# Input loads moved from SyncE's queue to ScalarE's, one batch's stacks sent later, and the idle matmuls placed behind a wait

## What is computed

```
xn = layernorm(x)
q, k, v = xn @ Wq.T + bq, ctx @ Wk.T + bk, ctx @ Wv.T + bv      # 16 heads of 16
z = softmax(q k^T) v  per head
x = x + layernorm(z + xn) * gamma + beta
f = layernorm(x);  f = f + mixture_of_experts(layernorm(f))      # 8 experts, top 2 of a softmax router
x = x + f
```

## Time and profile before

| | |
|---|---|
| median of three executions | 836.14 us (835.61 to 837.38) |
| profiled execution, and its span | 837.38 us, 835.5 us |
| TensorE busy | 752.3 us, 90% |
| VectorE busy | 629.9 us, 75% |
| ScalarE busy | 564.1 us, 68% |
| GpSimd busy | 536.1 us, 64% |
| DMA | 104.43 MB, mean 125 GB/s |
| chain that ended last | TensorE 58%, DMA 12%, VectorE 9%, GpSimd 6%, SyncE's queue 5% |

### The profile page before, as it was taken

One profiled execution on the slowest core, in us unless ns is written; L12 is line 12 of the kernel. 1 busy time (PEld: TensorE's weight loads), 2 busy tenths in 40 slices (PEclk: granted clock), 3 DMA queues, 4 the chain that ended last, 5 costly groups with the idle time before them and its releaser, 6 DMA issues.

```text
span 835.5 us, 26294 instructions
## 1 busy us (share of the span) xinstructions
PE 752.3 (90%) x8080; PEld 587.7 (70%) x8081; DVE 629.9 (75%) x1781; ACT 564.1 (68%) x1469; POOL 536.1 (64%) x609
## 2 busy tenths in 40 slices
PE   7888989999999999999999997555979888999994
PEld 4565666767777777777777674435878777999994
DVE  7688998989989999989999897784366763445441
ACT  3466767878888888888888785334565544666662
POOL 5433657767768767777777674335656555777773
PEclk9999999999999999999999999755989998999998
DMA  8566665777786786877877868511334323443341
GB/s 216 145 142 163 151 149 125 176 167 153 163 180 153 172 173 148 184 151 165 180 152 164 193 126 206 165 21 43 61 56 59 58 40 58 70 70 58 62 66 18
DMA packets 154001, 104.43 MB, mean 125 GB/s; under 512 B 68365, under 2 KB 149561, under 8 KB 153817
## 3 DMA queue, kind: packets, MB, share of 16 engines
q1 hardware_dynamic: 135502, 79.47, 43.3%
q0 software_dynamic: 10944, 14.10, 10.6%
q10 hardware_dynamic: 7498, 10.18, 4.1%
HBM read 36.65 MB, written 17.33 MB: 65 GB/s over the span
## 4 chain that ended last, share of the span: by engine, by line
PE 58%; DMA 12%; DVE 9%; POOL 6%; issue 6%; SPq 5%; ACT 2%; DVEq 1%; ACTq 0%; POOLq 0%
PE s_row L1004 9%; PE pj L899 7%; PE s_row L913 7%; PE zt L945 6%; PE s_t L933 6%; PE pj L868 6%; PE pj L1015 4%; PE zt L1015 4%; SPq L660 3%; DMA out_x<-index_space,idx_s 3%; DVE negmax L1390 2%; DMA q_stack<-m_part 2%; PE pj L886 2%; DMA zscr<-zn 2%; DMA stack_x<-k_part 2%
## 5 line engine op out<-in xcount | busy, mean ns | idle before, releaser
L1390 DVE TENSOR_REDUCE negmax<-s_row 100x1 f32<-100x361 f32 x512 | 250.9, 522 | 23.6 <-PE s_row L913 19.3
L1209 ACT ACTIVATE p_t<-s_t 128x400 f32<-128x400 f32 x384 | 188.0, 499 | 82.1 <-PE s_t L933 74.3
L913 PE MATMUL s_row<-stack_x,q_stack 125*128 125x361 bf16 x512 | 132.5, 319 | 16.5 <-DVE negmax L1390 8.6
L730 POOL DMA_INDIRECT out_x<-index_space,idx_s x57 | 91.3, 1601 | 77.1 <-ACT index_space L1194 35.4
L933 PE MATMUL s_t<-q_stack,stack_x 128*128 128x100 bf16 x1536 | 129.4, 211 | 11.0 <-ACT p_t L1209 7.9
L933 PEld LDWEIGHTS s_t<-q_stack,stack_x 128*128 128x128 bf16 x1536 | 94.5, 99 | 56.1 <-issue 31.3
L1004 PE MATMUL s_row<-w_qkv,v_aug 128*128 128x128 f32 x912 | 117.9, 285 | 1.7 <-DVE v_aug L1485 1.7
L1004 PEld LDWEIGHTS s_row<-w_qkv,v_aug 128*128 128x128 f32 x912 | 113.2, 202 | 2.3 <-DVE v_aug L1485 2.2
L1395 DVE TENSOR_SCALAR p_t<-p_t 128x1200 f32<-128x1200 f32 x128 | 100.8, 787 | 11.4 <-ACT p_t L1209 11.3
L899 PE MATMUL pj<-w_qkv,ct 128*128 128x256 f32 x384 | 104.8, 395 | 0.3 <-ACT k_rest L1130 0.3
L945 PE MATMUL zt<-p_t,v_aug 128*32 128x100 f32 (+1 forms) x3072 | 96.3, 260 | 0.8 <-DVE p_t L1395 0.8
(11 more groups left out here) (244 smaller groups left out, 1413.9 us busy)
## 6 DMA issues: line engine op xcount, KB each, us to landing
stack_x<-k_part SPq DMA_DIRECT2D x192, 192.0 KB, 3.6
q_stack<-q_part SPq DMA_DIRECT2D x192, 64.0 KB, 2.0
ct<-in_ctx_t SPq DMA_DIRECT2D x32, 361.0 KB, 4.3
stack_x<-in_w ACTq DMA_DIRECT2D x8, 512.0 KB, 6.4
w_s<-in_w ACTq DMA_DIRECT2D x14, 256.0 KB, 3.0
zscr<-zn SPq DMA_DIRECT2D x32, 100.0 KB
z_in<-zscr SPq DMA_DIRECT2D x32, 100.0 KB
zf_d<-zf_s SPq DMA_DIRECT2D x32, 100.0 KB
```

The costliest lines, as they stand in the source:

```text
L730: pool.indirect_dma_start(out_rows[0:n], bass.IndirectOffsetOnAxis(idx_s[:, k.slot:k.slot + 1], 0), ys[:, k.slot, :], None, bounds_check=n ...
L913: nc.tensor.matmul(s_row[h % 2][:, 0:KEYS], q_stack[0:MROW, b.slot, h, :], k_stack[0:MROW, b.slot, h, 0:KEYS], start=True, stop=True).then ...
L1209: nc.scalar.activation(p_t[:, quad % 2, kt, :], s_t[g % 2][:, 0:4 * Q], ACT.Exp).then_inc(exp_done, 1)
L1390: v.tensor_reduce(negmax[:, b.slot, h:h + 1], s_row[h % 2][0:Q, 0:KEYS], AXIS.X, ALU.max, negate=True).then_inc(max_done, 1)
```

## The change

Four edits. (1) The x loads 2 to 5 get the sizes 10, 3, 4 and 3 batches and are issued by ScalarE, in the slots (iteration, slot) = (-1, 8), (0, 2), (0, 8), (1, 2), ahead of what ScalarE has in that slot. (2) `first_stacks` sends batch 0 only; batch 1 goes by the places of SP like the later ones, in slot 2 of iteration -1. (3) The first key half of batch 0 goes to `pj[1]` instead of `s_t[0]`. (4) The idle matmuls write `tr` instead of `s_t[1]`, and TensorE's wait for the four memsets stands ahead of them.

```diff
-X_LOADS = [slice(0, FIRST), slice(FIRST, 12), slice(12, 17), slice(17, 22), slice(22, 27), slice(27, B)]
-X_LOAD_BEHIND = {1: 2, 2: 3, 3: 4, 4: 5}
+X_LOADS = [slice(0, FIRST), slice(FIRST, 12), slice(12, 22), slice(22, 25), slice(25, 29), slice(29, B)]
+X_LOAD_AT = {(-1, 8): 2, (0, 2): 3, (0, 8): 4, (1, 2): 5}
...
-                return (s_t[0], zt)[t] if a.known and a.index == 0 else pj[1]
+                return zt if a.known and a.index == 0 and t == 1 else pj[1]
...
-                def x_load(k):
-                    sp.dma_start(x_all[:, X_LOADS[k], :], x.rearrange("b q d -> q b d")[:, X_LOADS[k], :]).then_inc(x_loaded[k], 16)
-
-                def first_stacks(b):
+                def first_stacks():
...
-                for b in range(2):
-                    first_stacks(b)
-                x_load(X_LOAD_BEHIND[1])
+                first_stacks()
...
-                            if w.known and w.index < 2:
+                            if w.known and w.index == 0:
...
-                            if w.known and w.index in X_LOAD_BEHIND:
-                                x_load(X_LOAD_BEHIND[w.index])
...
-                        nc.tensor.matmul(s_t[1][:, 0:G * Q], zt_s[:, 0:128], zt_s[:], start=True, stop=True)
+                        nc.tensor.matmul(tr[:, 0:G * Q], zt_s[:, 0:128], zt_s[:], start=True, stop=True)
...
+                pe.wait_ge(memsets, 4)
                 pe.wait_ge(zeros_ready, 1)
                 run_idle(8)
-                pe.wait_ge(memsets, 4)
...
+                        if isinstance(turn, int) and (i, s) in X_LOAD_AT:
+                            k = X_LOAD_AT[i, s]
+                            act.dma_start(x_all[:, X_LOADS[k], :], xv[:, X_LOADS[k], :]).then_inc(x_loaded[k], 16)
```

More of the change, by code:

```diff
@@ L594, in _ @@
                 sp.wait_ge(pad_written, 3)
-                def x_load(k):
-                    sp.dma_start(x_all[:, X_LOADS[k], :], x.rearrange("b q d -> q b d")[:, X_LOADS[k], :]).then_inc(x_loaded[k], 16)
-                def first_stacks(b):
+                def first_stacks():
                     for part, (q_made, k_made, q_count, k_count) in enumerate(((qh_ready, kh_ready, 2, 2), (qm_ready, km_ready, 1, 1), (q_low_ready, k_low_ready, 1, 1))):
-                        sp.wait_ge(k_made, k_count * (b + 1))
+                        sp.wait_ge(k_made, k_count)
                         for g, p in enumerate(PROD):
                             if p == part:
-                                sp.dma_start(k_stack[g:ROWS:len(PROD), b].rearrange("r h k -> r (h k)"),
-                                             k_part[:, b, p].rearrange("p t k -> p (t k)")).then_inc(k_stacked[b], 16)
-                        sp.wait_ge(q_made, q_count * (b + 1))
+                                sp.dma_start(k_stack[g:ROWS:len(PROD), 0].rearrange("r h k -> r (h k)"),
+                                             k_part[:, 0, p].rearrange("p t k -> p (t k)")).then_inc(k_stacked[0], 16)
+                        sp.wait_ge(q_made, q_count)
                         for g, p in enumerate(QPART):
                             if p == part:
-                                sp.dma_start(q_stack[g:ROWS:len(PROD), b].rearrange("r h k -> r (h k)"),
-                                             q_part[:, b, p].rearrange("p t k -> p (t k)")).then_inc(q_stacked[b], 16)
-                for b in range(2):
-                    first_stacks(b)
-                x_load(X_LOAD_BEHIND[1])
+                                sp.dma_start(q_stack[g:ROWS:len(PROD), 0].rearrange("r h k -> r (h k)"),
+                                             q_part[:, 0, p].rearrange("p t k -> p (t k)")).then_inc(q_stacked[0], 16)
+                first_stacks()
                 def later_loads():
```

## The result

The changed kernel takes 846.01 us (median of six, 842.66 to 849.81) against 835.88 us of the kernel before beside it: ratio 1.0109, 95% interval 1.0087 to 1.0132. It is slower, by 9 to 10 us; the forecast was 838.2 us and the range ended at 842.0. The profiled execution after took 848.3 us, its span is 846.4 us, 10.9 us more than before. The work is the same: TensorE 751.0 us busy, VectorE 631.4.

What follows compares the result with a forecast made beforehand. The prediction took TensorE's pace to bound the kernel from about 140 us, so the first 110 us decide: 5.2 us later, 3.1 us regained, 836.14 + 2.1 = 838.2 us against the median; range 833.7 to 842.0 us.

Steps and rivals of the forecast that it cites:

- Idle matmuls behind the memsets: Kernel start: idle matmuls begin 3.94 us later, part comes back; 1.1 us late taken, ends 0 and 3.9.
- Batch 1's stacks: Before iteration 0: six key transfers wait for the low key part and land at 40 to 41, 3 to 4 us late.
- x load 2: Iteration 0 slot 1: VectorE gets the 1000 KB load at 44.9 instead of 39.68; 5.2 us late, earlier lateness included.
- The other loads: From 53.2 to 107 us: VectorE's x waits go and SP's queue is freed; 3.1 us gained, between 1 and 6.4.
- rival (d): Iteration 1: loads interleave with batch 2's stacks too, TensorE waits one more microsecond, 1 us back; 841.3 us; chance 0.07.
- (c): Start: the clock falls at batch 1 and load 2 lands at 46.3 or later; 840.9 us; chance 0.13.
- (a): Start: iteration 0's idle time, the zn store and `m_part` make delay and gain cancel; 836.1 us; chance 0.24.
- (b): Start: freeing SP's queue gains 6.4 us, load 2 lands early, stacks cost 3 us; 832.7 us; chance 0.14.
- The sum: Whole kernel: 837.38 + 5.2 - 3.1 = 839.5 us against the profiled execution, 838.2 us against the median; chance 0.42.

Runs made afterwards that it cites:

- the base: The kernel before with one difference: GpSimd's wait before a scatter in the second part takes its value by a load with bounds; ratio 0.9993 (0.9966 to 1.0020).

## Why the prediction was wrong

The direction was right and the size was not: 2.1 us were forecast, 10 came. By its steps:

- **Idle matmuls behind the memsets.** Right. Keys at 12.68 (forecast 12.9), the two subtractions 1.56 and 0.57 us, batch 1's key matmuls 1.40 us, lateness 0.5 us where 1.1 was forecast. The 1.3 us that the clock was to give back are 2.66 - 1.38 us, at a clock of 0.50 and at the full one; it did, with 1.40 us at 1.00. That the shorter gap kept the clock up is not shown: the base kept it too, with a gap of 1.70 us and no edit there.
- **Batch 1's stacks.** This step failed. It put the landing of the stacks at 40 to 41 us, with 1 to 2 us for the load and the context beside them. It was 46.7.
- **x load 2.** The sum of bytes was 2 to 3 us short: 43.9 us and 1 us to the semaphore, against 46.7 for the last of the stacks. No run shows that 1 us by itself: in the profile after, packets of SP's queue pass until 46.8 us and the rows start at 46.81. What failed is who waits. The step let VectorE's statistics, due at 39.68, wait for the load. In fact the load was the first to be through (its queue is empty after 44 us) and the stacks the last, and these are due at 37.35. The term was 5.2 us; it measured 46.81 - 37.35 = 9.5. Of the 4.3 us of error 2.3 are the earlier due time and the rest the later end.
- **Why the stacks were last.** The packets of both queues pass side by side, 271 of ScalarE's and 134 of SP's in 36 to 38 us of the profile after, and in the run with edit 1 alone even one 64 KB transfer was held for 8.9 us. Together they make a share of 1.12 until 40 us, and then only 0.75 and 0.69; with the load cut into 96 and 4 partitions the share stays at 1.1 until 44 us and 1.8 us come back. The prediction had the load beside the stacks, but gave that only the 1 to 2 us, and it let all bytes pass at the 231 GB/s of the earlier trace rows, where 185, 167 and 147 GB/s passed in the three stretches of 2 us from 40 us on.
- **The other loads.** VectorE's waits at 56, 72 and 78 us went, and iterations 2 and 3 gave back 2.9 us where 3.1 were forecast for all three. That the numbers agree is luck in part: half of the 3.1 was to come from the wait of 1.56 us in iteration 1, and that iteration takes 16.80 us where it took 16.77, since the clock of 0.90 cost the 1.3 us that the wait gave back. And iteration 0 lost 3.7 us: 3.0 of idle time, with a second wait of 3.05 us, and 0.7 of busy time at the lower clock. The prediction had no term for either. So the four iterations take 70.3 us, 0.9 more than the 69.5 before, where it wanted some 3 less. The second wait is rival (d), which had 0.07 and was priced at one microsecond; that loads beside batch 2's stacks hold them up was right (with loads 3 to 5 behind the stacks no wait of over 0.3 us is left there). (c) had the jam in view but capped the delay at 6.6 us, from twice the landing time of a load of half the size that was queued behind the stacks.
- **Rivals (a) and (b)** needed load 2 to land early or to be absorbed. Neither happened; the delay passed to the end undiminished, 10.5 us at batch 6 and 10.9 in the span.
- **The sum** with the measured terms: 9.7 + 3.7 - 2.9 = 10.5 us, and 0.4 in the rest.

Open: why the second wait was 3.05 us in one execution and 1.43 in another, and how much of the 10 us each edit makes by itself.

## What to carry to other kernels

In this kernel the large load that is not urgent does best on the queue of the urgent transfers, behind them, in a stretch in which the DMA engines are idle (0.9970 with each load one stack earlier); on another queue it is not behind them but among them (a wait of 8.68 us, and of 0.92 us with the load behind the stacks on SP's queue). What is issued behind it on its own queue waits for it in turn, as `m_part` did for 8.20 us, so the size has to fit the gap. When two transfers run together, cost both: ask which is through last, and whose consumer is due first. After a delay has been priced, ask also what its idle time does to TensorE's clock: here it was at 0.50 after 8.68 us of waiting, and the 197 matmuls of iteration 1 took 1.3 us longer at a mean of 0.90.

## What the runs showed of the hardware

With both queues in use, ScalarE's queue passed 271 packets to SP's 134 in 36 to 38 us and 165 to 163 in 38 to 40 us of the profile after; the ratio is not fixed, and why it changes is not shown. In bytes it was 0.28 to 0.18 MB and then 0.17 to 0.23 MB. And the same kernel start kept the full clock in one execution and lost it in another (1.40 and 2.66 us for four key matmuls), which moved `m_part` of batch 4 by 1.0 us. After a long wait the low clock cost TensorE more: 1.9 us of busy time in iteration 0 of the run with loads 3 to 5 on SP.
